# Two transposition groups moved back to TensorE, a new split of block moves between two queues, and a router fed before its 1/deviation is known

## The reference

```python
mod = (silu(c) @ wmod)                       # sa, ca, ga, sb, cb, gb
h = layernorm(x) * (1 + ca) + sa             # 16 heads of 64, causal attention over 2048 tokens
x = x + ga * attention(h)
h = layernorm(x) * (1 + cb) + sb
logits = h @ Wr.T + br                       # 8 experts
e = argmax(logits)
x = x + gb * (relu(h @ W1[e].T + b1[e]) @ W2[e].T + b2[e])
```

## Time and profile before

| | us |
|---|---|
| median of three executions | 979.15 |
| the three | 978.8, 984.84, 979.15 |
| the profiled execution, its own time | 988.01 |
| its span, from first to last instruction | 986.3 |
| PE / DVE / ACT / POOL busy in it | 913.3 / 761.9 / 633.8 / 422.6 |
| mean granted TensorE clock | 0.972 |

### The profile page before, as it was taken

How to read it: one execution, slowest core, us unless ns; L and a number is a source line. 1 busy time by engine, 2 the same in 40 slices (tenths; PEclk the granted TensorE clock), 3 DMA queues, 4 the chain that set the end, 5 groups by cost and what they waited for, 6 DMA issues and landing times.

```text
span 986.3 us, 19842 instructions
## 1 busy us (share of the span) xinstructions
PE 913.3 (93%) x6115; PEld 674.7 (68%) x6115; DVE 761.9 (77%) x2426; ACT 633.8 (64%) x1158; POOL 422.6 (43%) x765
## 2 busy tenths in 40 slices
PE   4999999989998999899998999899989999995796
PEld 3776767667675767677676767676767666773796
DVE  6898869875997769785988599867978689971463
ACT  4876668656774768665865677577857566551574
POOL 0274515442364316542554236431745144445054
PEclk9899999999999999999999999999999999986898
DMA  2035312342144302531245214430343013372120
GB/s 81 12 91 133 100 38 64 104 125 66 29 111 109 92 23 79 136 99 47 56 106 131 66 30 113 111 95 22 88 118 87 20 47 84 87 226 69 31 67 18
DMA packets 107211, 79.13 MB, mean 80 GB/s; under 512 B 32935, under 2 KB 94163, under 8 KB 107106
## 3 DMA queue, kind: packets, MB, share of 16 engines
q1 hardware_dynamic: 85378, 51.57, 19.7%
q0 software_dynamic: 21728, 26.29, 10.2%
HBM read 18.21 MB, written 11.77 MB: 30 GB/s over the span
## 4 chain that ended last, share of the span: by engine, by line
PE 59%; SPq 16%; DVE 12%; issue 5%; DMA 4%; ACT 2%; another core or an unknown queue 1%; POOL 1%; POOLq 0%; DVEq 0%; ACTq 0%
PE ps L940 18%; PE ps L899 13%; SPq L650 12%; PE ps L912 12%; PE ps L878 4%; DVE probs L1286 4%; DMA turned_far<-staged 3%; PE ps L882 3%; PE ps L1064 2%; DVE probs L1289 2%; PE ps L1075 2%; PE ps L953 2%; SPq L710 2%; SPq L699 2%; DVE staged L1303 1%
## 5 line engine op out<-in xcount | busy, mean ns | idle before, releaser
L650 POOL DMA_DIRECT2D turned_far<-staged x640 | 313.1, 497 | 353.4 <-DVE staged L1303 340.4
L1129 ACT ACTIVATE probs<-probs,neg_max 128x128 f32<-128x128 f32 (+15 forms) x256 | 308.7, 1207 | 151.2 <-DVE neg_max L1293 148.6
L899 PE MATMUL ps<-k_both,q_both 128*128 128x512 f32 (+2 forms) x1280 | 344.1, 393 | 12.9 <-DVE probs L1286 7.7
L899 PEld LDWEIGHTS ps<-k_both,q_both 128*128 128x128 f32 x1280 | 208.7, 190 | 84.9 <-issue 30.5
L1286 DVE TENSOR_SCALAR_CACHE_REDUCE probs<-ps 128x512 f32<-128x512 f32 (+1 forms) x384 | 243.4, 662 | 5.0 <-PE ps L899 4.0
L1137 ACT COPY pT<-ps 128x512 f32<-128x512 f32 (+1 forms) x341 | 177.1, 557 | 94.8 <-PE ps L912 76.3
L912 PE MATMUL ps<-ident,probs 128*128 128x128 f32 x1440 | 203.8, 278 | 2.3 <-ACT probs L1129 1.4
L912 PEld LDWEIGHTS ps<-ident,probs 128*128 128x128 f32 x1440 | 172.4, 143 | 46.5 <-issue 23.3
L940 PE MATMUL ps<-pT,v_sb 128*64 128x256 f32 (+1 forms) x1568 | 179.1, 370 | 5.7 <-DVE pT L1322 3.8
L940 PEld LDWEIGHTS ps<-pT,v_sb 128*64 128x64 f32 x1568 | 104.4, 137 | 74.0 <-issue 19.1
L1303 DVE STREAM_TRANSPOSE staged<-probs 128x640 f32<-128x640 f32 (+1 forms) x160 | 122.0, 778 | 37.6 <-DMA turned_far<-staged 15.9
(11 more groups left out here) (147 smaller groups left out, 700.7 us busy)
## 6 DMA issues: line engine op xcount, KB each, us to landing
turned_far<-staged POOLq DMA_DIRECT2D x384, 40.0 KB, 2.5
turned_far<-staged SPq DMA_DIRECT2D x384, 40.0 KB, 2.0
x_sorted<-blank SPq DMA_DIRECT2D x19, 458.5 KB, 5.3
rinv_b<-spread_rows SPq DMA_DIRECT2D x128, 64.0 KB, 2.7
turned_far<-staged SPq DMA_DIRECT2D x256, 32.0 KB, 1.9
turned_far<-staged POOLq DMA_DIRECT2D x256, 32.0 KB, 1.8
spread_rows<-rinv_rows SPq DMA_DIRECT2D x256, 0.5 KB
probs<-in_L_ffn_W_dram SPq DMA_DIRECT2D x1, 2048.0 KB, 11.6
```

Of the source, the lines that this page charges most:

```text
L650: queue.dma_start(turned_far[b * SQUARE:(b + 1) * SQUARE, m % FAR_BUFS, u, a, 0:far(g), :], staged[a * SQUARE:(a + 1) * SQUARE, u, b, 0:fa ...
L899: m = pe.matmul(ps_ring[:, s.bank, 0:w], q_split[r % 2][:, q0:q0 + P], k_split[r % 2][:, part, k0:k0 + w], start=(part == 0), stop=(part = ...
L1129: act.activation(row, row, ACT.Exp, bias=neg_max[:, g, r:r + 1], accum_out=row_sum[:, g, r:r + 1]).then_inc(exp_done, 1)
```

## The change

Five things are altered, and the order of all steps is worked out again by the planner with new costs.

1. `far` is zero for the last two groups of the last pair, (7,6) and (7,7): their first five tiles are turned on PE like the others. 38 moves are left.
2. In the second half (u = 1) of each move SP issues one step a = 0 and POOL issues three, a = 1, 2, 3 (12 of the 16 DMAs). The first half stays 8 and 8.
3. `fresh` only subtracts the mean. The 1/deviation is made in a step of its own, `rstds`, after it. `turn2` turns x minus mean, `mod2` is a plain copy, and `route` multiplies with the router's weights already scaled by 1+cb.
4. The part of the logits that is the same for all tokens (bias, and the shift through the router) is made once, early, by `const` and `consts`; `pick` applies 1/deviation and adds that row before its argmax. The bias matmul of each `route` goes.
5. SP reads two tile starts ahead (`EARLY_STARTS`) in place of four before it waits for the scatter.

```diff
+LAST_NEAR = 2
+HARD, SOFT = (128, 64), (128, 192)
 ISSUE = 650.0
+SOFT_ISSUE = 500.0
-def far(g):
-    return FAR.get(g, 0)
+def far(p, g):
+    return FAR.get(g, 0) if p * GROUPS + g < PAIRS * GROUPS - LAST_NEAR else 0
...
-            steps += [(self.move_at(m, u)[0] + 4 * ISSUE * i, "move", (p, g, u, 2 + i)) for u in range(2) for i in range(2)]
+            steps += [(self.move_at(m, u)[0] + 4 * SOFT_ISSUE * i, "move", (p, g, u, 2 - u + i)) for u in range(2) for i in range(2 + u)]
...
-                begin = max(begin, self.move_at(m if u else m - 1, 1 - u)[0] + 8 * ISSUE)
+                begin = max(begin, self.move_at(m if u else m - 1, 1 - u)[0] + (12 * SOFT_ISSUE, 8 * ISSUE)[u])
...
-            self.moved[m, u] = begin + HOP, begin + HOP + 8 * ISSUE + LAND
+            self.moved[m, u] = begin + HOP, begin + HOP + (8 * ISSUE, 12 * SOFT_ISSUE)[u] + LAND
...
-                for a in range(2):
+                for a in range(2 - u):
                     steps.append((self.move_at(m, u)[0] + 4 * ISSUE * a, "move", (p, g, u, a)))
...
-    EARLY_STARTS = 4
+    EARLY_STARTS = 2
...
-                                pe.wait_ge(moved[u], 128 * m_no + 128)
-                                pe.wait_ge(moved_soft[u], 128 * m_no + 128)
+                                pe.wait_ge(moved[u], HARD[u] * (m_no + 1))
+                                pe.wait_ge(moved_soft[u], SOFT[u] * (m_no + 1))
...
+                elif s.kind == "const":
...
+                    pe.matmul(ps_ring[:, s.bank, 0:NE], ones[:], br_row[:], start=True, stop=False, skip_group_check=True)
+                    pe.matmul(ps_ring[:, s.bank, 0:NE], ones[:], wr_shift[:], start=False, stop=True,
+                              skip_group_check=True).then_inc(bank_full[s.bank], 1)
...
-                    pe.matmul(ps_ring[:, s.bank, 0:n * NE], ones[:], br_row[:].unsqueeze(1).broadcast_to([P, n, NE]),
-                              start=True, stop=False, skip_group_check=True)
...
                         m = pe.matmul(ps_ring[:, s.bank, NE * t:NE * t + NE], hT[:, (first + t) * P:(first + t + 1) * P],
-                                      wrT[:], start=False, stop=True, skip_group_check=True)
+                                      wr_scaled[:], start=True, stop=True, skip_group_check=True)
...
-                    act.activation(hT[:, first * P:(first + n) * P], ps_ring[:, bank, 0:n * P], ACT.Identity,
-                                   bias=mod[:, 3:4], scale=mod[:, 7:8]).then_inc(bank_free[bank], 1)
+                    act.copy(hT[:, first * P:(first + n) * P], ps_ring[:, bank, 0:n * P]).then_inc(bank_free[bank], 1)
...
+                    dve.tensor_scalar(wr_scaled[:], wrT[:], mod[:, 7:8], None, ALU.mult)
+                    dve.tensor_scalar(wr_shift[:], wrT[:], mod[:, 3:4], None, ALU.mult).then_inc(bank_free[bank], 1)
...
+                    for t in range(first, first + n):
+                        m = dve.tensor_scalar(x_normed[:, t, :], x_sb[:, t, 0:E], mean_var[:, t, 0:1], None, ALU.subtract)
+                    m.then_inc(norm_ready, 1)
+                elif s.kind == "rstds":
...
-                    for t in range(first, first + n):
-                        m = dve.tensor_scalar(x_normed[:, t, :], x_sb[:, t, 0:E], x_sb[:, t, MEAN:MEAN + 1],
-                                              x_sb[:, t, RSTD:RSTD + 1], ALU.subtract, ALU.mult)
-                    m.then_inc(norm_ready, 1)
...
-                    link(dve.tensor_reduce(top[:, 0:n], logits, AX.X, ALU.max))
                     for t in range(n):
-                        m = dve.scalar_tensor_tensor(out=is_top[:, t, :], in0=logits[:, t, :], scalar=top[:, t:t + 1],
-                                                     in1=expert_no[:], op0=ALU.is_equal, op1=ALU.mult)
+                        m = dve.scalar_tensor_tensor(out=scores_of[:, t, :], in0=logits[:, t, :],
+                                                     scalar=x_sb[:, first + t, RSTD:RSTD + 1], in1=logit_0[:],
+                                                     op0=ALU.mult, op1=ALU.add)
                     m.then_inc(bank_free[bank], 1)
                     dve.wait_ge(bank_free[bank], use + 1)
+                    link(dve.tensor_reduce(top[:, 0:n], scores_of[:, 0:n, :], AX.X, ALU.max))
+                    for t in range(n):
+                        m = dve.scalar_tensor_tensor(out=is_top[:, t, :], in0=scores_of[:, t, :], scalar=top[:, t:t + 1],
+                                                     in1=expert_no[:], op0=ALU.is_equal, op1=ALU.mult)
+                    link(m)
```

More of the change, by code:

```diff
@@ L101 @@
 class Plan:
-    IN_RING = ("score", "out", "proj", "back", "small", "turn2", "route", "rank", "total", "wturn")
-    EMPTIES = {"top": "score", "lo": "proj", "value": "proj", "add": "out", "resid": "back", "smalls": "small",
+    IN_RING = ("score", "out", "proj", "back", "small", "const", "turn2", "route", "rank", "total", "wturn")
+    EMPTIES = {"top": "score", "lo": "proj", "value": "proj", "add": "out", "resid": "back", "smalls": "small", "consts": "const",
                "mod2": "turn2", "pick": "route", "slots": "rank", "ends": "total", "wtake": "wturn"}
@@ L126, in __init__ @@
                     add=norms, resid=ends,
-                    small=[(0, 0)], smalls=[(0, 0)], fresh=ends, turn2=ends, mod2=ends, route=ends, pick=ends,
+                    small=[(0, 0)], smalls=[(0, 0)], const=[(0, 0)], consts=[(0, 0)], fresh=ends, rstds=ends, turn2=ends, mod2=ends, route=ends, pick=ends,
                     rank=ends, slots=ends, total=[(PAIRS - 1, 0)], ends=[(PAIRS - 1, 0)],
@@ L167 @@
     CLOSING = ("out", "back", "turn2", "route", "rank", "total")
-    KINDS = dict(pe=("score", "turn", "pv", "out", "proj", "back", "small", "turn2", "route", "rank", "total", "wturn"),
+    KINDS = dict(pe=("score", "turn", "pv", "out", "proj", "back", "small", "const", "turn2", "route", "rank", "total", "wturn"),
                  act=("hi", "value", "take", "exp", "mod2", "wtake"),
-                 dve=("norm", "sum", "lo", "shuffle", "add", "resid", "top", "take", "smalls", "fresh", "pick", "slots", "ends"))
+                 dve=("norm", "sum", "lo", "shuffle", "add", "resid", "top", "take", "smalls", "consts", "fresh", "rstds", "pick", "slots", "ends"))
     FIRST = dict(act=("hi", "value"), dve=("sum", "norm", "lo"))
@@ L211, in ready @@
             if past and k0 < tiles_of(past[1]) * P:
-                behind = at("shuffle", past[0], past[1], key[2]) if far(past[1]) else 0.0
+                behind = at("shuffle", past[0], past[1], key[2]) if far(*past) else 0.0
                 over = min((k0 + w) // P, tiles_of(past[1])) - 1
-                if over >= far(past[1]):
+                if over >= far(*past):
                     behind = max(behind, at("turn", past[0], past[1], over))
@@ L234, in ready @@
             return at("resid", p, g)
+        if kind == "pick":
+            return max(at("route", p, g), at("rstds", p, g))
         if kind == "total":
@@ L242, in ready @@
         if kind in self.IN_RING:
[L243 removed]
+            return max(at({"const": "smalls", "turn2": "fresh", "route": "mod2", "rank": "pick"}[kind], *key), self.ring_free())
         return at({"hi": "proj", "lo": "hi", "add": "out", "resid": "back", "smalls": "small", "mod2": "turn2",
[L245 removed]
+                   "consts": "const", "rstds": "fresh", "slots": "rank", "ends": "total", "wtake": "wturn"}[kind], *key)
     def get_from(self, p, g):
@@ L332, in took @@
                 return 866.0 + switch
-            n = 1.0 if kind in ("small", "total") else parts_of(key[0])[key[1]][1] / 4.0
-            return n * {"out": 862.0, "back": 436.0, "small": 200.0, "turn2": 436.0, "route": 440.0,
+            n = 1.0 if kind in ("small", "const", "total") else parts_of(key[0])[key[1]][1] / 4.0
+            return n * {"out": 862.0, "back": 436.0, "small": 200.0, "const": 500.0, "turn2": 436.0, "route": 440.0,
                         "rank": 700.0, "total": 400.0}[kind] + switch
         if kind == "shuffle":
-            return far(key[1]) * P / 0.96 + 100.0
+            return far(*key[:2]) * P / 0.96 + 100.0
         if kind == "top":
@@ L1274, in _ @@
                     past = group_before(p, g, 2)
-                    if past and far(past[1]) and c == 0:
+                    if past and far(*past) and c == 0:
                         dve.wait_ge(shuffled, 4 * plan.move_no[past] + r + 1)
```

81 lines of the change are left out of this document (46 added, 35 removed).

## The result

| | before | after |
|---|---|---|
| median of the executions, us | 982.0 (978.8 to 985.66, 4 runs) | 938.32 (937.02 to 938.62, 4 runs) |
| the profiled execution, own time | 988.01 | 938.13 |
| its span | 986.3 | 936.4 |

The ratio is 0.9552, with a 95% interval from 0.9507 to 0.9596: 44 us faster, where 961 us had been forecast and 952 was the end of the range. The direction was right; of the 44 us the forecast had 18.

What follows compares the result with a forecast made beforehand. It took TensorE as the bound (PE busy 913.3 of 986.3 us). Subtracting 15.5, 10.8 and 0.6 from the profiled 988.0, or 15.5, 1.9 and 0.6 from the median 979.15, gave 961 us, range 952 to 971.

Steps and rivals of the forecast that it cites:

- Part 1: Moves' second halves: moving four of SP's eight DMAs to POOL saves 15.5 us, between 12 and 23.8.
- I take 15.5 of the 17.8: PE's 13 waits for moved blocks, 17.8 us in all: 15.5 go, leaving about 0.2 each.
- Part 2: Last two groups turned on TensorE: 10.8 us against the profiled execution, 1.9 against the median (5.3 to -3).
- an end at 898.8: End of the attention: 898.8 in place of 909.6 profiled; the median's end was put near 900.7.
- one stretch of 6.8 us at half clock: End of the attention: one PE stretch at half clock stays after the change, adding 3.4 us.
- hole of some 2.7 us: End of the attention: DVE's 14.68 us stop without a known releaser is only some 2.7 us in the median.
- Part 3: Router: a shorter chain brings the first sorted tile earlier, gaining 0.6 us, between 0 and 1.2.
- (a): Moved blocks: half the saved waits are given back as PE waits for DVE; 968.5 us, chance 0.16.
- (b): End of the attention: the hole stays in every execution, caused by the weights' load; 970 us, chance 0.10.
- (c): Moves: transfers, not issue, are the limit, so only parts 2 and 3 remain; 976.6 us, chance 0.03.
- (d): Moves: POOL becomes the late queue and DVE waits before its shuffles; 989 us, chance 0.05.
- (e): SP's queue: its put and get hold it back whatever follows, so the change does nothing; 977 us, chance 0.04.

Runs made afterwards that it cites:

- e1: Kernel before with only the split of the moves' second halves and the planner's costs for it; 959.17 us, ratio 0.9749.
- e2: Kernel before with the split of the moves but the planner's old costs, so the old order; 958.79 us, ratio 0.9734.
- e3: Kernel before with only the planner's new costs and order, 8 and 8 DMAs in both halves; 976.62 us, ratio 0.9895.
- e15: e1 with a wait before the ninth scatter on a semaphore that has long had its value; 945.97 us, ratio 0.9634.
- e14: e1 with the row of scatters cut: after eight, the rest wait for the last pv; 946.07 us, ratio 0.9652.
- e11: Changed kernel with only the last group turned on TensorE (LAST_NEAR = 1), (7,6) moved by DMA again; 943.84 us, ratio 0.9612.
- e6: Changed kernel with one more wait on GpSimd, so that twelve scatters stand in one row; 951.57 us, ratio 0.9689.
- e10: Changed kernel with four tile starts read ahead instead of two (EARLY_STARTS = 4); 938.89 us, ratio 0.9558.
- e12: Changed kernel with the last four groups turned on TensorE instead of two (LAST_NEAR = 4); 937.00 us, ratio 0.9548.
- e4: Changed kernel without the split of the moves and its planner costs; 977.83 us, ratio 0.9917.
- e17: e1 run again unaltered, on another chip, in the same call as e18; 958.78 us, ratio 0.9724.
- e18: e15 run again unaltered, on the same chip as e17; 958.01 us, ratio 0.9714.
- e5: e1 with the first two parts' scatters (8 of 16) placed between GpSimd's last moves; 947.14 us, ratio 0.9647.
- e8: e7 with the scatters of two parts spread between the moves as in e5; 948.49 us, ratio 0.9665.
- e7: Changed kernel with the last two groups moved by DMA again (LAST_NEAR = 0); 959.03 us, ratio 0.9759.
- e9: e1 with GpSimd's whole row of 14 scatters held back until the last pv; 956.12 us, ratio 0.9735.
- e13: e1 with the indirect scatters replaced by plain DMAs of the same rows to consecutive places; 943.45 us, ratio 0.9624.
- e16: e1 with the whole row of 14 scatters held until five pv steps are left; 951.42 us, ratio 0.9694.

## Why the prediction was wrong, step by step

It was wrong in two terms. Against the profiled execution's own time it subtracted 15.5, 10.8 and 0.6 from 988.0 and came to 961.1; measured is 938.1, 23 us less. Ahead of the cut 31.5 us were gained, 16.0 more than all of part 1 was given. Behind it 18.4 were gained, 7.0 more than parts 2 and 3 were given.

**Part 1: the mechanism right, the term half of what it is.** The prediction found the late queue, and what was to show it did: SP 4 DMAs, POOL 12 in 5.86 us, waits for blocks gone on PE, 0.3 us on DVE. The failed step is "I take 15.5 of the 17.8", with 17.8 plus six times 1.0 as the upper bound: it counted one row, PE's wait for the DMAs, and added its neighbours by guess. e1 measured 31.3 at the cut, all else as before. Up to there 21.0 us of PE's idleness went in the changed kernel, the waits for `top` with the waits for blocks: more than the 15.5, inside the bound of 23.8. The other 10.5 us isn't idleness at all, but PE's busy time, which the sum held constant. Half of it is TensorE's clock: behind a wait it ran for some 3.4 us at the lower level (1.2 GHz), as in the kernel before after the 3.46 us of the earlier trace rows; a window of before around it:

```profile
310.00:318.00 8.00, 5.20 (x26) 3.50 (x27) 3.63 (x9) 0.33 (x2) 2.58 (x6) 0.79 0.29 77
```

The mean granted clock up to the cut went from 0.99 to 1.00 [windows above]. In the kernel before three stretches up to the cut have the lower level, 13.6 us in all (at 30.1, 204.2 and 313.4); the changed kernel, e1 and e2 have one, of 3.4 us. 10.2 us less at half speed are some 5.1 us of busy time (an estimate from these stretches, with PE busy 13.0 of the 13.6 us). The rest goes with the order: e2, the split in the old order, and e1, in the new one, have the same 3.4 us at the lower level, and PE's busy time up to their cuts is 665.00 and 660.74. With the order alone (e3) it is 668.75, with 17.0 us at the lower level. The rows to ask were those of whole pairs. Two of before, from one cut to the next, and one of after:

```profile
284.10:392.80 108.70, 103.41 (x685) 74.08 (x684) 85.87 (x260) 72.10 (x127) 47.35 (x89) 0.98 0.32 82
392.80:498.20 105.40, 101.78 (x685) 73.32 (x684) 85.89 (x260) 72.13 (x127) 47.31 (x89) 1.00 0.33 84
```

```profile
273.80:373.80 100.00, 99.69 (x680) 72.30 (x676) 83.54 (x256) 71.79 (x128) 56.26 (x107) 1.00 0.35 89
```

The same work took 103.41 and 101.78 us of PE's busy time in two pairs, so that itself was open, and each pair was 3.6 to 5.3 us longer than it. Some 4.4 us in each of seven pairs is 31 us: the bound to give for idleness, and not the sum of one row. That it is also the 31.5 us measured is luck: 21.0 of these were idleness and 10.5 busy time. The 0.79 us for each DMA wasn't typical either: the earlier trace rows shows the slowest of the 14 second halves that SP issued in one piece (median 5.33 us for eight).

**Part 2: both sums too small, the one with the hole and the one without.** The end of the attention was put at 898.8 in place of 909.6, 10.8 us earlier, with 1.9 of them against the median. Counted from the cut, the last `out` starts after 200.7 us before and after 181.0 in the changed kernel: 19.7 less. Behind it the changed kernel takes 1.3 us more (77.2 against 75.9).

Most of the 19.7 is the hole, that is the stop (some 14 us, by the next number). On D, where it is absent, e15 has the same split and none of part 2, and its last `out` starts 186.3 us after the cut. What part 2 gives there is 5.3 us ahead of the last `out` and 4.2 behind it, 9.5 in the profiles and 8 in the medians' ratios (0.9634 to 0.9552, on different chips); against e14 on C it is 1.6 and 5.7. On chip B, one group near, then two, then four: 943.84, 938.89, 937.00. Part 2 was to give between -3 and 5.3 against the median: exceeded.

The failed step is the term of 1.9 us, "an end at 898.8" against one "near 900.7". Two things in it were mis-sized. First, it kept "one stretch of 6.8 us at half clock" on the way. The changed kernel has none there: from 811 to 852 PE is busy 40.98 of 41.00 us at a granted clock of 1.00, where e15 has two such stretches of 6.8 us (at 811.4 and 845.6). Its last `pv` ends 179.6 us after the cut, where 189.1 was forecast (898.8 less 709.7), and e15's 185.7.

Second, it had no term behind the attention, and there GpSimd ends the program. The last instruction of GpSimd is a DRAIN, and the span goes on behind the last packet of its DMAs: 9.23 us in all twelve runs where it issues the moves of all groups with the split, 7.61 with one group near (e11), 5.97 with two (the changed kernel, e6, e10), 3.68 with four (e12), and without the split 5.97 (before, e3) and 3.36 (e4). These 3.3 us, which the split costs and part 2 gives back, no sum had. What the time goes by isn't shown; the number of DMAs issued alone doesn't order it (679 before and 799 in the changed kernel have the same 5.97).

The "hole of some 2.7 us" in the median isn't borne out either. The prediction took the hole for an accident of single executions. By their times e1 (956.4 to 960.7), e17 and e18 have it in every execution on A and E, and e15 (944.0 to 946.9) in none on D, and it costs 12 us there. Whether the changed kernel took it away or ran on a chip without it isn't settled: its chip isn't known, and its nearest variants (e10 to e12) ran on B. Its scatters stand in rows of 8, 4, 2 and 2, and on A the stop went or shrank in such an order (e5, e8), though a row of 8 in e4 still had one of 6.8 us.

On D, without the stop, the medians divide the gain without any cut: 35.2 us from before to e15, where part 1 was given 15.5, and 8 from there to the changed kernel, where parts 2 and 3 were given 2.5.

**Part 3: right.** It was given 0.6; e7 against e1, e8 against e5 and e10 against the changed kernel show 0 within 1.4. As predicted, the first sorted tiles are read from 875.68, before DVE copies its first expert at 877.14; they were read from 927.76 and copied from 926.37 before.

**The rivals.** (a) came true only where the split was missing (e3). (b): the hole did stay in e1, e2, e3 and e7, and took back 10 to 12 us in e1 and e7, but for another cause than the weights. (c) falls with e1. The rule of the Trainium skill, page DMA: Bandwidth & Descriptors, section Rules for kernel authors, says that spreading DMAs over the engines saves only the sequencer's issue time. These runs agree, and that issue time was worth 27 us in e1: up to the cut the DMAs' share was 0.31 before and 0.33 after, so it wasn't bandwidth that the split brought. (d) falls: POOL is busy 58.6 us more and waits 185.6 us for DVE. (e) falls with the timeline.

**What was to show it.** "The busy time of PE should rise by 3 to 6 us" was wrong in sign, by the 10.5 us above and by 8.2 behind the cut; DVE fell by 7.6 and not by 3.

## What to carry to other kernels

A wait that recurs in every period is priced by the period, not by its own row: compare the length of a period with the bound engine's busy time in it, at full clock, and give that difference as the upper bound of the idle time; the clock behind each wait comes on top. Compare the issue time of a batch of small DMAs with its landing time: here the issue was the longer. For a hole without a named releaser, look for a signal of a neighbouring engine that came late, run the same kernel on a second chip, and compare kernels on one chip only. And look at what stands between the last landed output and the end of the program.

## What the runs showed of the hardware

**A stop that depends on the chip or the group of runs.** While GpSimd issued 14 indirect DMAs of 128 rows, one in 1.26 us, TensorE's signals came up to 12.1 us late on E (e18) and up to 14.2 on A (e1), and the engines that wait for them stood; on D PE worked on (17.08 of 17.50 us), and likewise on B and C, in nearly the same program. On A the stop went or shrank when the row was broken (e5, e8). So there the row is part of the cause; what differs between the chips or groups, and why only TensorE's signals are late, stays open. The clock isn't it (0.88 granted in the window, where DVE and ACT do a sixth of their work), nor the DMAs' bandwidth (61 GB/s against 62). Nor is it the loading of instructions or weights: from 859 to 884 us of e18 the only packets of any queue are GpSimd's. e9, e11, e13, e14 and e16 were run on chips without the stop, so they don't tell whether a later row, a shorter row or plain DMAs would avoid it. The kernel before lost less between such chips: its medians are 985.98 on E and 981.15 on D.

**GpSimd at the end of the program.** Behind the last packet of its DMAs the span goes on for 3.4 to 9.2 us, the same to 0.02 us in every run with the same moves (9.23 in e1 and e15, 5.97 in the changed kernel), while GpSimd's DRAIN runs.

**Issue costs.** SP's issue of one DMA of a move took 0.59 us in the median, before and after, with single ones of up to 1.9: four took 2.41 us, the eight of the earlier trace rows 6.29, of which two issues took 1.04 and 1.43. POOL took 0.49 for each (5.86 for twelve), with 1.26 for an indirect one.
